# A decoder layer on one Trainium2 core: rotated queries, exponentials ahead of the clipping, and the mask as a TensorE product

## What is computed

```python
q = _apply_rope((x @ Wq)...); k = _apply_rope((x @ Wk)...)   # 16 query heads, 4 key heads, 128 wide
s1 = q[..., :64] @ k[..., :64].T / 8      # first map
s2 = q[..., 64:] @ k[..., 64:].T / 8      # second map
allowed = (j <= i) & (j >= i - 63)        # others are set to -1e30
a1, a2 = softmax(s1), softmax(s2)
diff = relu(a1 - lam * a2)
out = (diff / (sum(diff) + 1e-6)) @ v
x = x + concat(out) @ Wo
```

## Time and profile before

| | before |
|---|---|
| median of 3 runs | 1332.57 us (1331.23 to 1333.62) |
| the profiled execution | 1330.37 us |
| its span, first to last instruction | 1328.5 us |
| mean granted TensorE clock | 0.991 |
| TensorE busy | 1256.6 us, 95% |
| VectorE, ScalarE, GpSimd busy | 836.5, 720.2, 468.3 us |

### The profile page before, as it was taken

One profiled execution on the slowest core, in us unless ns is written; L12 is line 12 of the kernel. 1 busy time (PEld: TensorE's weight loads), 2 busy tenths in 40 slices (PEclk: granted clock), 3 DMA queues, 4 the chain that ended last, 5 costly groups with the idle time before them and its releaser, 6 DMA issues.

```text
span 1328.5 us, 27286 instructions
## 1 busy us (share of the span) xinstructions
PE 1256.6 (95%) x9584; PEld 990.3 (75%) x9584; DVE 836.5 (63%) x1986; ACT 720.2 (54%) x2746; POOL 468.3 (35%) x451
## 2 busy tenths in 40 slices
PE   5799999999999788999999999988999999999998
PEld 4578888888887565666666666567888888888887
DVE  6788888888888676666666656776343443433433
ACT  2788888788888753444444544464332332323322
POOL 3122112212221125454543634641153352533532
PEclk9999999999999989999999999999999999999999
DMA  6002000200012101202103101200335341143340
GB/s 223 17 18 56 18 17 18 57 18 17 17 34 91 33 16 43 82 18 90 35 17 99 25 17 33 76 1 1 111 81 131 63 131 47 39 143 74 57 93 32
DMA packets 34737, 72.78 MB, mean 55 GB/s; under 512 B 7872, under 2 KB 12992, under 8 KB 33344
## 3 DMA queue, kind: packets, MB, share of 16 engines
q1 hardware_dynamic: 34624, 71.32, 20.1%
HBM read 52.29 MB, written 2.23 MB: 41 GB/s over the span
## 4 chain that ended last, share of the span: by engine, by line
PE 74%; DVE 10%; ACT 8%; issue 4%; POOL 2%; DMA 1%; SPq 0%; DVEq 0%; POOLq 0%; ACTq 0%
PE ps L553 33%; PE ps L946 9%; PE ps L669 5%; PE ps L701 4%; PE ps L833 3%; ACT ea L1457 3%; PE ps L739 3%; PE ps L815 3%; PE ps L843 2%; PE ps L692 2%; PE ps L823 2%; PE ps L608 2%; ACT ea L1501 2%; DVE ea L1095 1%; PE ps L683 1%
## 5 line engine op out<-in xcount | busy, mean ns | idle before, releaser
L1830 POOL TENSOR_TENSOR sg<-sg,cw 128x512 f32<-128x512 f32 x88 | 113.8, 1293 | 260.0 <-ACT sg L1620 256.8
L1398 DVE TENSOR_TENSOR hh<-ps,sg 128x512 f32<-128x512 f32 x100 | 69.1, 691 | 178.8 <-POOL sg L1830 161.2
L1424 ACT ACTIVATE hhh<-hh 128x512 fp32r<-128x512 f32 x100 | 63.3, 633 | 213.8 <-DVE hh L1398 211.6
L1457 ACT ACTIVATE ea<-ps,negmax 128x64 f32<-128x64 f32 (+1 forms) x512 | 165.0, 341 | 6.0 <-DVE negmax L1150 6.0
L1424 ACT ACTIVATE pt<-ps 128x512 f32<-128x512 f32 x128 | 77.1, 602 | 165.8 <-PE ps L823 109.6
L1197 DVE TENSOR_TENSOR qcs<-ps,tabb 128x512 f32<-128x512 f32 x192 | 123.5, 685 | 64.6 <-PE ps L553 64.0
L553 PE MATMUL ps<-xnh,wch 128*128 128x512 f32 x400 | 157.3, 393 | 0.0
L553 PE MATMUL ps<-xnl,wch 128*128 128x512 f32 x400 | 157.1, 393 | 0.0
L553 PE MATMUL ps<-xnh,wcl 128*128 128x512 f32 x400 | 155.7, 389 | 0.0
L1688 POOL TENSOR_TENSOR ea<-ea,rden 128x128 f32<-128x128 f32 (+1 forms) x128 | 62.3, 509 | 261.5 <-DVE rden L1106 261.5
L1695 POOL TENSOR_TENSOR eb<-eb,rsum 128x512 f32<-128x512 f32 x64 | 67.1, 1048 | 177.5 <-DVE rsum L1241 177.4
(11 more groups left out here) (154 smaller groups left out, 3298.1 us busy)
## 6 DMA issues: line engine op xcount, KB each, us to landing
raw_w<-in_rawb_dram SPq DMA_DIRECT2D x4, 2432.0 KB, 9.0
kva<-ktmp SPq DMA_DIRECT2D x64, 128.0 KB, 2.4
kvt<-qcs SPq DMA_DIRECT2D x64, 128.0 KB, 2.3
cw<-comb_d SPq DMA_DIRECT2D x32, 256.0 KB, 4.9
raw_w<-in_rawc_dram SPq DMA_DIRECT2D x4, 1920.0 KB, 7.9
cw<-comb_d SPq DMA_DIRECT2D x16, 224.0 KB, 4.8
raw_a<-in_wqk_dram SPq DMA_DIRECT2D x4, 768.0 KB, 5.7
cw<-comb_d SPq DMA_DIRECT2D x16, 192.0 KB, 5.6
```

Of the source, the lines that this page charges most:

```text
L1398: dve.tensor_tensor(hh[:, par, :], bank(C_U[par]), sg[:, par, :], ALU.mult).then_inc(c_h, 1)
L1424: return act.activation(dst, src, ACT.Copy)
L1457: last = act.activation(dst(m, h), src, ACT.Exp, bias=negmax[:, par, i:i + 1], accum_out=sums[:, par, i:i + 1])
L1830: pool.tensor_tensor(sg[:, par, :], sg[:, par, :], cw[:, c % 2, t, :], ALU.mult).then_inc(c_hs, 1)
```

## The change

1. **Rotated queries.** The query is rotated whole: `a_take` writes the query times the cosines into `qab[:, par, 0]` and times the sines into the other chunk's second half; SyncE crosses the sines' halves with two DMAs per query head (in place of four per chunk for the key); GpSimd adds both (`a_queries`, `a_qr`), and `a_keys` writes `kva` directly. A score product now contracts 64 rows and writes 64 partitions, so it uses a quarter of the array. There are still 16 per unit.
2. **The mask.** Two TensorE products (identity times `maskb`, 128x384, bfloat16) start each unit's score banks. ScalarE's copy of the mask is gone.
3. **Orders.** ScalarE runs the exponentials of n ahead of the clipping of n-1. VectorE takes the maximum of unit n directly after the addition to x, then the low part, `a_rec2`, `a_ratio`, `a_rho`, then slot(0), then `a_diff`. The buffers between (`ea0`, `sums`, `rec2` and others) grow from 2 to 4.
4. **Slots.** The items are k, q0, q1, q2, q3, v at (0,0), (0,1), (1,0), (1,1), (2,0), (3,0). Before, k, q0, q1, q2, v, q3 stood at (0,1), (1,0), (1,1), (2,1), (3,0), (3,1).

```diff
-        A_ITEMS = ["k", "q0", "q1", "q2", "v", "q3"]
+        A_ITEMS = ["k", "q0", "q1", "q2", "q3", "v"]
-        A_SLOT = {(0, 1): 0, (1, 0): 1, (1, 1): 2, (2, 1): 3, (3, 0): 4, (3, 1): 5}
+        A_SLOT = {(0, 0): 0, (0, 1): 1, (1, 0): 2, (1, 1): 3, (2, 0): 4, (3, 0): 5}
...
# SyncE
-                    sp.wait_ge(a_k, g * NC + c + 1)
-                    for m in range(2):
-                        for at in (0, 64):
-                            sp.dma_start(kva[at:at + 64, c % 2, m, :], ktmp[64 * m:64 * m + 64, 0, :]).then_inc(a_kd, 16)
+                    for h in range(HG if g or c else 0):
+                        sp.wait_ge(a_pf, (g * NC + c) * AW + (h + 2))
+                        for to, at in ((64, 0), (0, 64)):
+                            sp.dma_start(qab[to:to + 64, 1 - c % 2, 1, h, :], qab[at:at + 64, c % 2, 1, h, :])\
+                              .then_inc(a_qx[h], 16)
...
# TensorE, a_unit
-                        pe.wait_ge(a_kd, 64 * (g * NC + (c + 1)))
-                    wait(pe, a_mk, n - 1)
+                        pe.wait_ge(a_k, g * NC + (c + 1))
+                        pe.wait_ge(a_qr, HG * (g * NC + (c + 1)))
+                    wait(pe, a_ex, n - 1)
                     tok = slice(S * j, S * (j + 1))
                     for m in range(2):
-                        sc = A_S[u % 2][:, m, 0:SW]
-                        if first and u < 2:
-                            pe.matmul(sc, idb[:, :], maskb[:, :], start=True, stop=False, skip_group_check=True)
-                        for at, to, keys in ((QH, late(sc), S), (0, early(sc), QH)):
-                            for h in range(HG):
-                                rows = slice(QH * (h % 2), QH * (h % 2) + QH)
-                                last = pe.matmul(to[rows, h // 2, :],
-                                                 qab[:, c % 2, m, h, S * j + at:S * j + at + QH],
-                                                 kva[:, c % 2, m, S * j:S * j + keys],
-                                                 start=False, stop=at == 0, skip_group_check=True)
+                        pe.matmul(A_S[u % 2][:, m, 0:SW], idb[:, :], maskb[:, :], start=True, stop=False,
+                                  skip_group_check=True)
+                    for at, part, keys in ((QH, late, S), (0, early, QH)):
+                        for m, h in ((0, 0), (1, 1), (0, 1), (1, 0), (0, 2), (1, 3), (0, 3), (1, 2)):
+                            rows, d = slice(QH * (h % 2), QH * (h % 2) + QH), slice(64 * m, 64 * m + 64)
+                            last = pe.matmul(part(A_S[u % 2][:, m, 0:SW])[rows, h // 2, :],
+                                             qab[d, c % 2, 0, h, S * j + at:S * j + at + QH],
+                                             kva[d, c % 2, 0, S * j:S * j + keys],
+                                             start=False, stop=at == 0, skip_group_check=True)
...
# VectorE, a_take: the sines, crossed by two half-height products in the first chunk only (turns > 1)
-                for dst, tab in to:
-                    last = dve.tensor_tensor(quads(dst), src, bcast(taba[:, tab, :]), ALU.mult)
+                dve.tensor_tensor(quads(qab[:, par, 0, h, :]), src, bcast(taba[:, 0, :]), ALU.mult)
+                if turns == 1:
+                    last = dve.tensor_tensor(quads(qab[:, par, 1, h, :]), src, bcast(taba[:, 1, :]), ALU.mult)
...
# ScalarE, a_unit: exps(...) stands ahead of the Relu loop, and this goes:
-                if not drain and not (final and u >= UN - 2):
-                    act.wait_ge(a_ex, n + 1)
-                    copy(A_S[u % 2][:, :, 0:SW], maskb[:, :].unsqueeze(1).broadcast_to([128, 2, SW])).then_inc(a_mk, 1)
...
# GpSimd
-                pool.tensor_tensor(ktmp[:, 0, :], ktmp[:, 0, :], ktmp[:, 1, :], ALU.add).then_inc(a_k, 1)
+                pool.tensor_tensor(kva[:, c % 2, 0, :], ktmp[:, 0, :], ktmp[:, 1, :], ALU.add).then_inc(a_k, 1)
+            def a_queries(g_to, c, heads):
+                for h in heads:
+                    if isinstance(g_to, int) and g_to == 0 and c == 0:
+                        pool.wait_ge(a_pf, h + 2)
+                    else:
+                        pool.wait_ge(a_qx[h], 32 * (g_to * NC + c))
+                    q = qab[:, c % 2, 0, h, :]
+                    pool.tensor_tensor(q, q, qab[:, 1 - c % 2, 1, h, :], ALU.add).then_inc(a_qr, 1)
+            A_TURNED = [(), (0,), (1, 2), (3,)]
```

More of the change, by code:

```diff
@@ L682, in a_unit @@
                     for p in range(XP):
-                        pe.transpose(quads(bank(PTB))[0:QH, p, :], early(ea[:, u % 2, 0, :])[:, p, :], idf[:, :])
+                        pe.transpose(quads(bank(PTB))[0:QH, p, :], early(ea0[:, (u - 2) % 4, :])[:, p, :], idf[:, :])
                     for p in range(XP):
-                        last = pe.transpose(quads(bank(PTB))[:, XP + p, :], late(ea[:, u % 2, 0, :])[:, p, :], idf[:, :])
+                        last = pe.transpose(quads(bank(PTB))[:, XP + p, :], late(ea0[:, (u - 2) % 4, :])[:, p, :], idf[:, :])
                     last.then_inc(a_tp, 1)
@@ L1043, in a_take @@
                 if item == 0:
-                    wait(dve, a_kd, 64 * chunk)
+                    wait(dve, a_k, chunk)
                     dve.tensor_tensor(quads(ktmp[:, 0, :]), src, bcast(taba[:, 4, :]), ALU.mult)
@@ L1126, in a_unit @@
                 if two:
-                    a_den(n - 2, u % 2)
-                    a_rden(n - 2, u % 2)
+                    a_den(n - 2, (u - 2) % 4)
+                    a_rden(n - 2, (u - 2) % 4)
                 if not (first and u < 4):
                     add_x((u - 4) % UN, a_wo, n - 4, a_y)
-                if one:
-                    a_rec2(n - 1, (u - 1) % 2)
-                    a_ratio(n - 1, (u - 1) % 2)
-                slot(0)
-                if one:
-                    a_rho(n - 1, (u - 1) % 2, g if u else g - 1)
-                if not (first and u < 3) and not (drain and u >= 3):
-                    dve.wait_ge(a_o, n - 2)
-                    wait(dve, a_wo, n - 4)
-                    dve.tensor_tensor(by_head(oal[:, (u - 3) % 2, :, :]), by_block(bank(OB)),
-                                      by_head(oah[:, (u - 3) % 2, :, :]).bitcast(f32), ALU.subtract).then_inc(a_ol, 1)
-                if one:
-                    a_diff(n - 1, (u - 1) % 2)
                 if not drain:
@@ L1151, in a_unit @@
                        .then_inc(a_mx, 1)
+                if not (first and u < 3) and not (drain and u >= 3):
+                    dve.wait_ge(a_o, n - 2)
+                    wait(dve, a_wo, n - 4)
+                    dve.tensor_tensor(by_head(oal[:, (u - 3) % 2, :, :]), by_block(bank(OB)),
+                                      by_head(oah[:, (u - 3) % 2, :, :]).bitcast(f32), ALU.subtract).then_inc(a_ol, 1)
+                if one:
+                    a_rec2(n - 1, (u - 1) % 4)
+                    a_ratio(n - 1, (u - 1) % 4)
+                    a_rho(n - 1, (u - 1) % 4, g if u else g - 1)
+                slot(0)
+                if one:
+                    a_diff(n - 1, (u - 1) % 4)
                 if u == 3 and not drain:
@@ L1446, in a_take_v, with exps @@
                 copy(quads(kva[:, c % 2, 2, :]), quads(bank(PJ - AV % turns))).then_inc(a_vf, 1)
-            def exps(n, u, maps, mx, ex, free, dst):
-                par = u % 2
+            def exps(n, u, maps, mx, ex, dst):
+                par, to = u % 2, u % (2 * maps)
                 act.wait_ge(mx, n + 1)
-                wait(act, free, n - 1)
                 for m in range(maps):
@@ L1494, in a_unit @@
                     copy(pt[:, u % 2, :, :], quads(bank(PTB))).then_inc(a_pt, 1)
+                if not drain:
+                    wait(act, a_tp, n - 3)
+                    wait(act, a_df, n - 1)
+                    exps(n, u, 2, a_mx, a_ex, lambda m, h: a_blocks((ea1[:, u % 2, :] if m else ea0[:, u % 4, :]))[h])
                 if not (first and u < 1) and not (drain and u >= 1):
                     act.wait_ge(a_df, n)
[L1498 to L1500 removed]
+                    par = (u - 1) % 4
+                    for h, e in enumerate(a_blocks(ea0[:, par, :])):
                         last = act.activation(e, e, ACT.Relu, accum_out=rsum[:, par, h:h + 1])
                     last.then_inc(a_re, 1)
[L1503 to L1504 removed]
                 slot(1)
@@ L1556, in b_unit @@
                 if not drain:
-                    exps(n, u, 1, b_mx, b_ex, b_tp, lambda m, h: eb[:, u % 2, h, :])
+                    wait(act, b_tp, n - 1)
+                    exps(n, u, 1, b_mx, b_ex, lambda m, h: eb[:, u % 2, h, :])
                 slot(1)
@@ L1717, in a_unit @@
                     return
[L1718 to L1720 removed]
+                if final and c == NC - 1:
                     return
```

61 lines of the change are left out of this document (33 added, 28 removed).

## The result

The changed kernel takes 1518.59 us (median of 4 runs, 1516.78 to 1520.14) against 1332.38 us before (4 runs): 1.140 times as long, 95% interval 1.138 to 1.142, or 186 us more. The prediction was 1488 us with a range of 1440 to 1525. The sign, the mechanism and the range held; the centre was 31 us low.

What follows compares the result with a forecast made beforehand. The prediction took TensorE as the bound (busy 39.57 of 40 us). To the profiled 1330.4 us it added 124 for waits and 32 for the clock, giving 1486, or 1488 against the runs' median; range 1440 to 1525.

Steps and rivals of the forecast that it cites:

- The large term: TensorE ahead of slot(1): waits for VectorE's late take of slot(0), 3.86 us in j = 0 and 3.04 in j = 1.
- The block: Mask and score products of a unit on TensorE: 1.36 us (1.26 to 1.47), 0.13 less than the 1.49 before.
- The bare waits ahead of the product with v: TensorE in j = 2 and 3, slot(1) empty: waits for ScalarE's copy of the transposes, 0.94 us, twice a chunk.
- Sum of the waits: First attention, TensorE's waits less the shorter score blocks: 8.26 us more per chunk, 124 us over 15 chunks.
- The clock: TensorE's granted clock falls after the new slot(1) gaps, two per chunk, 30 in all: 32 us lost.
- I take two in three: 20 x 1.6: Of 30 slot(1) gaps on TensorE, 20 are followed by a clock fall costing 1.6 us each: 32 us.
- "all of them" bound: Upper bound for TensorE's clock: all 30 gaps followed by a fall, 4 us at half speed each, 60 us.
- The prediction's one case for a clock that holds: In the earlier trace, TensorE's granted clock was still 1.00 after an idle gap of 2.19 us.
- "The clock holds": Rival: the same TensorE waits in slot(1), but no fall of the clock behind them; 1457 us, chance 0.27.
- "TensorE doesn't wait in slot(1)": Rival: slot(0)'s take is done within 0.38 us of the scores' end, so the kernel is faster; 1321 us, chance 0.03.
- "The crossed sines arrive late": Rival: each chunk's first scores wait for the crossed sines, 36 us more; 1524 us, chance 0.04.
- "The quarter products overlap only two at a time": Rival: scores stay at 1.49 us and the mask adds 0.45, 35 us more; 1523 us, chance 0.04.

Runs made afterwards that it cites:

- The kernel with work in the gaps: The changed kernel with 28 (j = 0) and 22 (j = 1) unused products added on TensorE ahead of the slot(1) projection: 1470.76 us.
- third experiment: The changed kernel with items moved to k (0,1), q0 (1,0), q1 (1,1), q2 (2,0), q3 (2,1), v (3,1), VectorE's order kept: 1469.94 us.
- the kernel with both ahead and the moved slots: The changed kernel with slot(0)'s take and the low part ahead of VectorE's maximum, and the slots of the third experiment: 1370.65 us.
- the kernel with the old orders: The changed kernel with VectorE's and ScalarE's orders of the kernel before and the slots of the third experiment: 1399.11 us.

## Why the prediction was right, and what it sized wrong

**The large term held.** "VectorE takes the item of slot(0) after it has waited for this unit's scores": moving that one line ahead gave back 124 us, and moving it behind them in the kernel before made it 46 us slower. Waits of 3.86 and 3.04 us were worked out, from start to start. In the same terms they are 279.48 - 275.07 - 0.38 = 4.03 and 254.44 - 250.93 - 0.38 = 3.13 (275.07 and 250.93 are the starts of the transposes); the 3.78 and 2.89 in the timeline's brackets count only from the end of the last product. Step by step, the start of VectorE's maximum to that of the low part took 0.93 (251.07 to 252.00), the low part 0.60, the three small ones 0.50, each as read in the earlier trace rows.

**The block was at its lower bound.** Predicted 1.36 (1.26 to 1.47), measured 1.26: the 16 records of 64 keys take about half of what 16 of 128 keys take. The scores' 0.83 is the 0.60 of the earlier trace rows plus 0.23. The Trainium skill (TensorEngine Tiling, Instruction Overhead) says that a product of one column takes as long as one of 60. The prediction read this as if 64 columns then took as long as 128, which the page does not say, since 64 lie above its 60; the 1.26 us do not contradict it.

**The bare waits ahead of the product with v had the right place and the wrong releaser.** I had 0.94 us on ScalarE's `pt`; they were 262.77 - 260.87 - 0.38 = 1.52 us in the same terms (1.27 in the timeline's bracket), on VectorE's `oal`. I had followed the operand and not the bank that the product writes. With the low part ahead of the maximum, what remained was ScalarE's, 0.69.

**A wait was missed.** `wol`, once per group, 1.47 us ahead of the output projection: 0.4 us a chunk. VectorE's subtraction stands behind the maximum and the take as well.

**Sum of the waits.** 4.03 + 3.13 + 2 x 1.52 + 1.47 / 4 = 10.6 us a chunk. Off go 4 x 0.23 for the shorter block, 4 x 0.1 because the mask product also starts 0.1 us sooner behind the product ahead of it than the scores did (0.23 for 0.32 us behind a projection), and 0.2 of waits that the kernel before had itself. That leaves 9.0, where 8.26 was predicted: over 15 chunks 135 for 124. This part was good to 9%, partly by luck: the longer waits (1.4 us a chunk more, and 0.4 for `wol`) and the larger savings (1.0) go against each other.

**The clock is the term that was mis-sized.** Score blocks of j = 0 at 79.71 and at 591.62 us are 13 chunks apart: 39.4 us each, where the prediction had looked for 35. The same 13 chunks before (63.46 to 411.08) take 26.7 each, so a chunk is 12.6 us longer. 9.0 of them are the waits; 3.6 are left, 54 us in 15 chunks, where 32 was put. The step that failed was "I take two in three: 20 x 1.6". Of the 27 gaps between 60 and 600 us 26 were followed by projections longer than at full clock. What one costs can be read directly, from the first product of slot(1)'s projection to the first one behind the output projection. TensorE's timeline behind a gap with the fall, and the row that ends the stretch behind the one gap of 27 without (it starts at 254.44, shown above):

```profile
242.91 0.71 PE L558 MATMUL ps<-xnh,wah 128*128 128x512 f32 x1 [3.78 <-DVE ktmp L1053]
...
248.28 0.40 PE L558 MATMUL ps<-xnh,wah 128*128 128x512 f32 x1
...
258.22 0.40 PE L558 MATMUL ps<-xnh,wah 128*128 128x512 f32 x1
```

That is 5.37 us with the fall, and 3.78 us (254.44 to 258.22) without, so 1.6 us here; over all 27 gaps the same stretch, less the waits inside it, takes 5.64 us on average, 1.9 us lost per gap. Behind the gap before 279.48, in 2-us stretches:

```profile
280.00:282.00 2.00, 2.00 (x6) 1.31 (x6) 1.97 (x5) 0.37 (x3) 0.79 (x1) 0.64 0.00 0
282.00:284.00 2.00, 2.00 (x7) 1.33 (x6) 1.17 (x4) 1.70 (x8) 0.71 (x2) 0.50 0.00 0
```

30 x 1.9 = 57 us is near the "all of them" bound of the prediction, 60. So the count was off most (26 of 27 for two in three) and the price a little (1.9 for 1.6). The prediction's one case for a clock that holds, the gap of 2.19 us, was read rightly although the row lies mostly inside the gap: from 36 to 42 us the granted clock is 1.00 too. But it was no guide, since gaps of 2.21 us in the kernel with the take late were followed by a fall. The kernel with work in the gaps, 48 us faster at a clock of 0.98, shows by experiment that this is the clock and not another wait.

The whole then adds up. From the first scores to those of the last chunk the changed kernel is 184.7 us longer (15 x 12.6 would be 189; the first and the last chunk differ less); the start is 3.5 us late (first scores at 33.26 instead of 29.75), near the 4 that the prediction charged it, and the last chunk is 1.6 us shorter. Together 187. The waits were 11 us over the prediction and the clock 22; the range held because its high end had the fall behind every gap.

**The rivals.** "The clock holds" (1457) falls with the two rows above. "TensorE doesn't wait in slot(1)" falls too; and the kernel in which it hardly waits there, with the take first, is at 1394 and not at 1321: the estimate of 1321 forgot that the other waits stay. "The crossed sines arrive late" falls: no wait of TensorE in the steady part names them, and they land in 2.3 us. "The quarter products overlap only two at a time" falls with the 0.83.

**What the orders do together.** The change's gain, a block 0.23 us shorter, is the sum of 0.66 saved on scores and 0.43 paid for a mask that ScalarE had written in time that cost nothing. That is 0.9 us of a chunk. Against that every arrangement tried brought 2.8 us or more of new waits per chunk, as slots, low part, norm and value copy now have less room. This holds for the arrangements tried, and does not show that none would win.

## What to carry to other kernels

When a consumer's list is reordered, look at every single buffer that it empties: an instruction that frees a bank must not stand behind a wait for work that the producer puts after the bank's next use. A releaser may belong to the bank written as well as to the operand read, so ask of each product for both. And a wait of 2 to 4 us on TensorE costs more than its length: here each wait of 2.9 to 3.8 us cost 1.9 us more on average through the clock.

## What the runs showed of the hardware that was not expected

**The length of a gap alone does not decide about the clock.** In the changed kernel 26 of 27 gaps of 2.86 to 3.96 us were followed by products longer than at full clock. With the moved slots (third experiment) it was 14 of 28, between 2.86 and 4.13 us, and two gaps of the same 2.89 us went either way. TensorE's timeline of that kernel:

```profile
244.04 0.50 PE L558 MATMUL ps<-xnh,wah 128*128 128x512 f32 x1 [2.89 <-DVE qab L1061]
244.38 0.39 PE L558 MATMUL ps<-xnl,wah 128*128 128x512 f32 x1
...
267.47 0.80 PE L558 MATMUL ps<-xnh,wah 128*128 128x512 f32 x1 [2.89 <-DVE qab L1061]
268.06 0.63 PE L558 MATMUL ps<-xnl,wah 128*128 128x512 f32 x1
```

In the kernel before with the take late, even gaps of 1.76 us were followed by longer products in some places (318.91) and not in others (409.99), and one of 2.19 us in the kernel before itself was not the earlier trace rows. What decides stays open; no run isolates it.

**VectorE and GpSimd hold each other up on SBUF operands.** In the kernel with both ahead and the moved slots, VectorE's `den` beside GpSimd's addition of the key:

```profile
249.91 1.11 DVE L1112 SCALAR_TENSOR_TENSOR den<-sums,rsum 128x4 f32<-128x4 f32 x1 [0.28 <-ACT ea L1513]
249.72 1.29 POOL L1690 TENSOR_TENSOR kva<-ktmp 128x512 f32<-128x512 f32 x1 [5.13 <-DVE ktmp L1053]
```

`den`, 0.15 us in the changed kernel, took 1.11 us and ended within 0.01 us of the addition (251.02 and 251.01). In the changed kernel `a_diff`, 1.00 us at 254.30, took 2.12 at 242.88, where GpSimd's addition ran from 242.93 to 244.20. The takes and the maximum, which read PSUM, kept their times. The Trainium skill (SBUF — State Buffer, SBUF: two separate sides) says that a VectorE operation with two SBUF inputs and a GpSimd operation that reads SBUF share a pair of ports, which the first to start holds to its end. The trace of `den` agrees, with these numbers. For `a_diff` it agrees that one waits for the other, but not on which: by the records its first instruction started 0.05 us ahead of the addition, and the addition still kept its 1.27 us. In the changed kernel no wait of TensorE names this chain, and behind the `den` shown here TensorE did not wait for the norm either. In the kernel with the old orders `a_diff` took 2.79 us beside GpSimd's additions and was on the way to the late copy of the value.
